# One block for attention, weight composition and feed-forward, with overlaid buffers and six early primitive pairs

## What is computed

```python
def _compose_weight(logits, A, B):
    vals, idx = jax.lax.top_k(logits, 32)
    w = jax.nn.softmax(vals)
    return jnp.einsum('k,kir,kro->io', w, A[idx], B[idx])
W1 = _compose_weight(fc1_logits, fc1_A, fc1_B)   # (256, 1024), rank 64
W2 = _compose_weight(fc2_logits, fc2_A, fc2_B)   # (1024, 256), rank 64
h = jax.nn.gelu(jnp.einsum('bsd,df->bsf', x, W1))
x = _layernorm(x + jnp.einsum('bsf,fd->bsd', h, W2))
```

## Time and profile before

| | us |
|---|---|
| median of 3 runs (lowest, highest) | 1985.33 (1983.23, 1987.44) |
| the profiled execution's own time | 1980.46 |
| its span, first to last instruction | 1978.6 |
| last attention output product to first composed pair, TensorE | 1091.8 to 1113.1 |
| composition, 32 pairs, TensorE | 1113.1 to 1214.0 |
| first product of the feed-forward | 1221.5 |

### The profile page before, as it was taken

The page is one execution under the profiler, slowest core; times in us unless marked ns, Lnnn a source line. Parts: engine busy times, 40 slices in busy tenths (PEclk is TensorE's granted clock), DMA queues, the critical chain, the costliest instruction groups (busy, mean ns, idle before and its releaser), DMA issues. The chain is left out here.

```text
span 1978.6 us, 47563 instructions
## 1 busy us (share of the span) xinstructions
PE 1921.4 (97%) x19760; PEld 1578.4 (80%) x19760; DVE 1344.3 (68%) x3293; ACT 981.7 (50%) x1803; POOL 1074.4 (54%) x1002
## 2 busy tenths in 40 slices
PE   8998999999999999999999699999999999999998
PEld 2335888888888888888888478999999999999997
DVE  3555566676667766776667465768696968677776
ACT  4454666676667666766676354223233232223231
POOL 1453998899888998899889111212222121313221
PEclk9997999999999999999999899999999999999999
DMA  7344200022000300021000694101010101010100
GB/s 273 122 162 166 105 34 34 34 76 76 34 34 8 112 34 34 34 76 55 34 24 20 187 239 102 43 22 43 22 44 33 38 28 44 22 44 22 44 11 22
DMA packets 26247, 128.04 MB, mean 65 GB/s; under 512 B 4592, under 2 KB 5168, under 8 KB 19888
## 3 DMA queue, kind: packets, MB, share of 16 engines
q1 hardware_dynamic: 17776, 78.08, 11.7%
q0 software_dynamic: 4624, 34.67, 5.7%
q10 hardware_dynamic: 3632, 12.26, 1.6%
HBM read 93.53 MB, written 31.46 MB: 63 GB/s over the span
## 5 line engine op out<-in xcount | busy, mean ns | idle before, releaser
L31 PE MATMUL bankC<-down_hi,act_hi 128*128 128x256 f32 x1024 | 289.5, 283 | 0.0
L33 PE MATMUL bankC<-down_hi,act_lo 128*128 128x256 f32 x1024 | 287.1, 280 | 0.0
L32 PE MATMUL bankC<-down_lo,act_hi 128*128 128x256 f32 x1024 | 286.9, 280 | 0.0
L1463 DVE TENSOR_TENSOR act_lo<-gel,act_hi 128x512 fp32r<-128x512 f32 x256 | 210.6, 823 | 8.8
L31 PE MATMUL bankC<-aT_hi,up_hi 128*128 128x512 f32 x512 | 204.9, 400 | 1.4 <-DVE aT_lo L1452 1.4
L1425 POOL TENSOR_TENSOR rstdC<-var_epsC,minus_halfC 128x4 f32<-128x4 f32 x48 | 53.6, 1117 | 278.4 <-DVE var_epsC L1488 278.4
L33 PE MATMUL bankC<-aT_hi,up_lo 128*128 128x512 f32 x512 | 202.1, 395 | 0.0
L32 PE MATMUL bankC<-aT_lo,up_hi 128*128 128x512 f32 x512 | 201.4, 393 | 0.0
L32 PEld LDWEIGHTS bankC<-down_lo,act_hi 128*128 128x128 f32 x1024 | 192.9, 188 | 1.4
L31 PEld LDWEIGHTS bankC<-down_hi,act_hi 128*128 128x128 f32 x1024 | 192.9, 188 | 1.4
L33 PEld LDWEIGHTS bankC<-down_hi,act_lo 128*128 128x128 f32 x1024 | 192.7, 188 | 0.0
(11 more groups left out here) (195 smaller groups left out, 5436.5 us busy)
## 6 DMA issues: line engine op xcount, KB each, us to landing
w_first<-w_split POOLq DMA_DIRECT2D x8, 1536.0 KB, 7.2
w_second<-w_split POOLq DMA_DIRECT2D x8, 1536.0 KB, 8.0
xs<-in_x_conv SPq DMA_DIRECT2D x16, 513.0 KB, 7.6
u<-hA SPq DMA_DIRECT2D x8, 1024.0 KB, 4.3
u_next<-u SPq DMA_DIRECT2D x8, 1024.0 KB, 5.4
u<-yB SPq DMA_DIRECT2D x8, 1024.0 KB, 4.6
hC<-u SPq DMA_DIRECT2D x16, 512.0 KB, 3.9
xC<-in_x SPq DMA_DIRECT2D x16, 512.0 KB, 4.2
```

Source lines behind the costliest of these rows:

```text
L31: e.matmul(out, wh, xh, start=start, stop=False)
L32: e.matmul(out, wh, xl, start=False, stop=False)
L33: return e.matmul(out, wl, xh, start=False, stop=stop)
L1463: e.tensor_tensor(a_lo[:, fb, :], g, a_hi[:, fb, :].bitcast(F32), ALU.subtract).then_inc(s_act_lo, 1)
```

## The change

- Attention, composition and feed-forward become one block. Each phase function returns its five engine programs (`Programs`), and each engine runs attention's, which then calls the next phase's. The wait of all engines between these phases is gone; instead an engine waits for named counts (`wait_free(w, before.free[...])`) before it uses memory that attention used.
- Buffers are laid over each other (`overlay`): three more raw buffers lie on the attention's tables `cos_k`, `sin_k`; `duo_hi` on `hT`; `duo_lo` on `gkT` and `kc`; `xC` and `hC` on `cos_q`, `sin_q`. PSUM: the first weight's banks are `ring`'s, the second's `big`'s; the feed-forward takes its banks in an order by which its first six are freed one after another.
- The ring of raw pairs has 6 buffers, all six loaded before the composition, three of them once the last unit's keys are rotated (`s_ks`). All halves are loaded by SyncE; GpSimd loads none.
- Unit 31 is finished between the pairs.
- ScalarE stores the last sequence after pair 11, and loads `b1s` and `vec` after pair 12, once that store has landed.
- Eight opening matmuls become four, ahead of pair 16; the first weight's banks are opened by their first matmul.
- The bias product comes after pair 22, and the first transposes and their split after pair 29.
- In `conv_phase`, three of the four semaphores of `band2` are shared with those of `band1`, so the first use of a part waits for both tables of it.

```diff
+            w.wait_ge(s_mul, 2 * (UNITS - PAIR + 1) + 2)
+            w.wait_ge(s_v, 4 * (UNITS - LANES))
+            prefetch(e, (0, 1, 2))
+            w.wait_ge(s_ks, 4 * UNITS)
+            prefetch(e, (3, 4, 5))
+            store(UNITS - LANES)
+            then(e)
...
+            def last(g):
+                if g == 0:
+                    copy_out(UNITS - 1)
+                    return
+                for o in range(4 * g - 4, 4 * g):
+                    unit(UNITS - 1, o)
+                if g == 2:
+                    w.wait_ge(s_unit, 8 * UNITS)
+                    n = UNITS - 1
+                    e.dma_start(rows_of(u_out, batch_of(n)), y_of(n)[:, :, :]).then_inc(d_sent[lane(n)], 16)
...
-                        if n == 5 + 4 * k + 2 * part:
+                        if n == 8 + 4 * k + 2 * part:
+                            wait_free(w, before.free["tables of q"])
...
-                    if n == 20 + 2 * s:
-                        e.wait_ge(d_u4[0], 16)
-                        e.dma_start(flat(hs[s]), pick(h_rows, 0, s)).then_inc(d_h[s], 16)
+                    if n == 26 + 2 * s:
+                        w.wait_ge(d_u4[0], 16)
+                        w.wait_ge(s_w_lo, 1)
+                        w.wait_ge(s_b1_ps, 1)
+                        e.dma_start(rows(hs[s]), pick(h_rows, 0, s)).then_inc(d_h[s], 16)
...
+            def scalar_loads(e, w):
+                wait_free(w, before.free["all"])
                 e.dma_start(b1s[:, :], b1).then_inc(d_consts, 16)
                 e.dma_start(vec[:, :], rows2.partition_broadcast(P)).then_inc(d_consts, 16)
...
+        FINISH = {2: 0, 3: 1, 4: 2, 6: 3, 7: 4, 8: 5}
+        UNITS_AT = {7: 1, 11: 2}
+        FIRST_AT = {14: 0, 22: 1}
+        TAKE_AT = DUOS + 2
+        BIAS_AT = DUOS + 6
+        ROWS_AT = len(duos) - 3
...
+            for n in range(RAW, len(duos)):
+                w.wait_ge(s_lo, n - RAW + 1)
+                for half in range(2):
+                    load_half(e, comp, picks, *duos[n], half, raw[n % RAW], d_raw[n % RAW])
+                first.sync(e, w, n)
...
+            wait_free(w, before.free["ring"])
+            for n in range(len(duos)):
+                if n == DUOS:
+                    w.wait_ge(s_zero, 1)
+                    wait_free(w, before.free["big"])
+                    for i in range(4):
+                        e.matmul(acc[1][i][:, :], zero[:, 0:P], zero[:, :], start=True, stop=False)
+                multiply(n)
+                if n == 0:
+                    last()
+                if n == BIAS_AT:
+                    w.wait_ge(s_out_lo, 4)
+                    first.tensor_bias(e, acc[0][0])
+                if n == ROWS_AT:
+                    w.wait_ge(s_out_lo, 4)
+                    rows()
...
+            wait_free(w, before.free["hT"])
+            for n in range(len(duos)):
+                prepare(n)
+                if n == 0:
+                    last(0)
+                if n in UNITS_AT:
+                    last(UNITS_AT[n])
+                if n == 12:
+                    first.scalar_loads(e, w)
+                if n in FIRST_AT:
+                    first.scalar(e, FIRST_AT[n])
+                if n == TAKE_AT:
                     take(0)
+            rows()
             take(1)
...
+        with nc.Block() as block:
+            block.sync(sync)
+            block.gpsimd(gpsimd)
+            block.tensor(tensor)
+            block.scalar(scalar)
+            block.vector(vector)
```

More of the change, by code:

```diff
@@ L1 @@
 import math
+from collections import namedtuple
 import concourse.bass as bass
@@ L1153, in ffn_phase @@
-def ffn_phase(nc, x, u_in, out, w1, b1, w2, rows2, comp, identity, w_col, picks, early, d_early, d_u4, x1_at, y_at):
+                invert(n)
+            key_value(UNITS - 1)
+            copy_turned(UNITS - 1)
+            then(e, lambda k: finish(UNITS - 1, k))
+        free = {"hT": [(s_v, 4 * UNITS)], "gkT, kc": [(s_kt, 4 * UNITS), (s_kr, 4 * UNITS)],
+                "tables of q": [(s_qr, 3 * UNITS), (s_qd, UNITS)], "ring": [(s_kvr, UNITS)], "big": [(s_y, 4 * UNITS)],
+                "all": [(s_unit, 8 * UNITS)] + [(d, 16 * (B // LANES)) for d in d_sent]}
@@ L1154, in ffn_phase @@
+        return Programs(sync, gpsimd, tensor, scalar, vector, free)
+def ffn_phase(nc, x, u_in, out, w1, b1, w2, rows2, comp, identity, w_col, picks, place, sems, before, early,
+              d_early, d_u4, x1_at, y_at):
     B, T, H = x.shape
@@ L1262, in ffn_phase @@
         aT = [split(f"aT{s}", [P, CB, TOK]) for s in range(LANES)]
-        act = [split(f"act{s}", [P, FB, TOK]) for s in range(LANES)]
+        act = [(place["act0_hi"], place["act0_lo"]), (place["act1_hi"], sb("act1_lo", [P, FB, TOK], F32R))]
         stats = sb("statsC", [P, LANES, TILES, 6])
@@ L1645, in scalar, with prepare @@
+        def scalar(e, last, rows):
             w = Waits(e)
-            first.scalar_loads(e)
-            def prepare(f, j):
-                n = duo_no(f, j)
+            def prepare(n):
+                f, j = duos[n]
                 r, q = n % RAW, n % SPLIT
                 w.wait_ge(s_mm, n - SPLIT + 1)
-                if n < len(early):
+                if n < RAW:
                     w.wait_ge(d_early[n], 2 * 16)
-                later = n // RAW + (r >= len(early))
-                for half in range(2):
-                    w.wait_ge(d_half[half][r], 16 * later)
+                else:
+                    w.wait_ge(d_raw[r], 2 * 16 * (n // RAW))
@@ L1695, in take, with overlay @@
                                     ALU.subtract).then_inc(s_out_lo, 1)
-            for f, j in duos:
-                prepare(f, j)
-                if (f, j) == (0, 10):
-                    first.vector(e, 0)
-                if (f, j) == (1, 2):
+            wait_free(w, before.free["gkT, kc"])
+            for n in range(len(duos)):
+                prepare(n)
+                if n in FINISH:
+                    last(FINISH[n])
+                if n in FIRST_AT:
+                    first.vector(e, FIRST_AT[n])
+                if n == TAKE_AT:
                     take(0)
-                if (f, j) == (1, 6):
-                    first.vector(e, 1)
+                if n == BIAS_AT + 2:
+                    first.vector_bias(e, acc[0][0])
+            rows()
             take(1)
-            first.vector_bias(e, acc[0][0])
-        with nc.Block() as block:
-            block.sync(sync)
-            block.gpsimd(gpsimd)
-            block.tensor(tensor)
-            block.scalar(scalar)
-            block.vector(vector)
+        free = [(first.done, 1), (s_out_lo, 4)] + [(s_out_lo, 4 + i) for i in range(1, 5)]
+        return Programs(sync, gpsimd, tensor, scalar, vector, free)
+def overlay(nc, stack, place, uses):
+    for use in uses:
+        own = stack if use is uses[-1] else ExitStack()
+        for name, shape, kind in use:
+            place[name] = own.enter_context(nc.sbuf_tensor(name, shape, kind))
+        if own is not stack:
+            own.close()
 def build(nc, t):
@@ new lines, in build @@
+        overlay(nc, ctx, place, [[("xC", [P, 2, T // P // 2, H], F32), ("hC", [P, 2, T // P // 2, H], F32)],
+                                 [("cos_q", split_rows, F32), ("sin_q", split_rows, F32)]])
+        d_u4 = [ctx.enter_context(nc.semaphore(f"d_u4_{s}")) for s in range(2)]
+        late = place["raw_late"]
+        early = [flat(u_next)[:, 0:width], w_flat[:, 0:width], w_flat[:, width:2 * width]] + [late[:, j, :] for j in range(3)]
+        d_early = [ctx.enter_context(nc.semaphore(f"d_early{j}")) for j in range(6)]
```

361 lines of the change are left out of this document (166 added, 195 removed).

## The result

| | before | after |
|---|---|---|
| median of 8 runs each (lowest, highest) | 1984.09 (1980.60, 1987.44) | 1974.70 (1971.98, 1977.99) |
| ratio, 95% interval | | 0.9955 (0.9944 to 0.9966) |
| the profiled execution's own time, span | 1980.46, 1978.6 | 1973.82, 1972.0 |
| end of unit 31's outputs | 1091.8 | 1090.8 |
| pair 0 starts on TensorE | 1113.1 | 1090.8 |

The change is 9.4 us faster. The forecast was 21.5 us, so the sign and the main mechanism held and the size did not: 1974.70 lies just outside the range of 1952 to 1974. The path from the end of the outputs to the feed-forward's first product went from 129.7 to 120.8 us, where 109.8 was forecast; and the feed-forward, forecast to keep its length, got longer.

A forecast was written before the change was run, and what follows sets the result against it. It took TensorE and DMA as two close limits in the composition. Terms summed to a path of 109.8 us against 129.7; with 1.6 from the feed-forward, 21.5 less than 1985.3: 1964 us, range 1952 to 1974.

The forecast's parts named there:

- The added wait on ScalarE: Composition, pairs 13 and 15: waits for the store, then `vec`, leave gaps of 4.4 and 3.2, together 7.6 us.
- I take 7: ScalarE's store of the last sequence: assumed to land 7 us after issue, so at 1130.0.
- rival 2: ScalarE's store queues behind SyncE's pairs and lands in 12.9: 13.5 instead of 7.6, total 1970 us; chance 0.20.
- Clock: TensorE in the composition: about 4 us at half clock after a gap cost 2.0 us, from nothing to 4.
- I count one: Clock losses in the composition: only one counted, 2.0 us; the first lies inside the wait of pair 15.
- It keeps its length: Feed-forward, TensorE busy from 1226 us: nothing the change touches runs there, so its 722 us stay unchanged.
- VectorE between pairs: Composition: in six places VectorE needs 3.1 to 3.4 against 2.77 us; costed at nothing, 1 to 2 without cover.
- SyncE's queue: SyncE waits for the bias product with pairs 27 to 31 queued behind: a gap of 1.6 us at pair 29.
- (1): Everything is covered: the store lands in 4, pairs are ahead, terms 7.6, 2.0 and 1.6 go; 1953 us, chance 0.12.
- (3): One queue carries less: SyncE alone moves 208 GB/s, 21.9 MB take 105.3 us; total 1973 us, chance 0.09.
- (4): Slower: SyncE's one queue moves only 164 GB/s, 133.5 us of transfer; total 2001 us, chance 0.03.
- (5): The gap only moves: pair 1 or freed buffers wait for unit 31; within 4 us of before, chance 0.03.

The follow-up runs named there:

- e6: Changed kernel with `b1s` and `vec` in memory of their own, loaded by SyncE with the early pairs, the store waited for after pair 14; 1959.72 us, ratio 0.9897.
- e4: Kernel before the change with only a 32-byte pad ahead of `act`, so `act` and `down` begin at the same place modulo 64; 1987.64 us, ratio 1.0024.
- e5: Changed kernel with `b1s` and `vec` in memory of their own, loaded by ScalarE without waiting for the store, which is waited for after pair 14; 1970.89 us.
- e7: As e6, with w1 rounded after pair 17 instead of 14; 1958.90 us, ratio 0.9886 to the kernel before the change.
- e9: Changed kernel with w2's halves loaded after pairs 20 and 22 instead of 12 and 14, and split at pair 26 instead of 22; 1968.96 us, ratio 0.9931.

## Why the prediction was right in kind and wrong in size

Its steps, against the changed kernel's trace:

| term | forecast us | measured us |
|---|---|---|
| wait ahead of pair 0 | 0.2 | 0 |
| 32 pairs | 90.6 | 90.9 (what is left of the path) |
| turn back and pair 1 | 2.4 | 2.3 (1093.65 to 1095.91) |
| idle ahead of pairs 12, 13, 15 | 0 + 4.4 + 3.2 | 1.3 + 7.9 + 7.3 |
| slow clock: pair 13, pair 15, behind the bias product | 2.0 | 2.0 + 1.5 + 1.5 |
| opening matmuls, bias product | 0.9 + 3.6 | 0.9 + 3.5 |
| gap ahead of pair 29 | 1.6 | 0 |
| transposes | 0.9 | 0.8 |
| gap ahead of pair 31 | 0 | 1.0 |
| path | 109.8 | 120.8 |
| the feed-forward's own length | 0 | +5.1 |

- **The added wait on ScalarE** is the step that failed by most: 7.6 forecast, 15.1 at pairs 13 and 15. The mechanism was right, both places and both releasers. The size failed in "I take 7" for the store and 6.6 for `vec`. The 6.6 came from a transfer issued with one of SyncE's ahead of it, and the earlier trace rows was read as showing that a later transfer is served at once. It showed the share once served. What the runs showed in its place is a wait for the first packet, 5.4 us for the store, followed by 4.9 us of transfer. The 7 did not follow from the forecast's own rule either: half of 244 GB/s is 122, so 1.05 MB take 8.6 us before any latency. Once served, the store had 68% of the engines, more than that half; rival 2's queueing was real too, but stopped after 5.4 us. The truth lay between the forecast and rival 2 for the store (10.3, between 7 and 12.9), and near rival 2 for `vec` (12.2). e6 confirms that these landings made the gaps: with `vec` loaded early and the store waited for only after pair 14, 12.5 us of idle time and slow clock went.
- **Clock**: the cost of one loss was about right, 1.5 to 2.0 us, but "I count one" failed: there were three, 5.0 us. Both gaps had one behind them. With the gaps forecast at 4.4 and 3.2, against the 1.96 us of the earlier trace rows behind which the clock had fallen, two should have been counted (gaps of about 2 us go either way: in e4 one of 2.10 had a loss behind it, 1.96 and 2.37 had none). The third came behind the bias product. The sum took the low clock of the transposes and of the cold start as gone, but what lies behind that product met it again in its new place, in all but one of the ten kernels with the new order. That the product causes it is read from rows; no run took it away.
- **"It keeps its length"**, said of the feed-forward, failed: +5.1 us. The argument was that nothing the change touches runs there. But the change touches where its operands lie, and a TensorE at 100% feels 1.7 ns a matmul. e4 shows it with a pad alone, 4.1 us in that stretch.
- **VectorE between pairs, costed at nothing**: 1.3 us at pair 12 and 1.0 at pair 31. Both came where GpSimd worked beside VectorE: GpSimd's two small operations after the last measurement took 1.51 and 1.56 us (0.24 and 0.23 on average before), and the norm's passes were waiting for them (the 1.75 us at 1121.71); and the subtraction of 2.61 us. The cover was thin by then, as ScalarE had waited 1.75 us for the load of pair 11, and 3.40, 1.31 and 1.78 us for those of pairs 29 to 31. Neither was taken away in a run, so these causes are read from rows only.
- **SyncE's queue** was priced too high: no gap at pair 29. The DMA's idle stretch was there, and the load of pair 29 was late for ScalarE by 3.40 us, but pairs were further ahead than assumed.
- **The start, the pairs, the opening matmuls, the bias product, the transposes** held within 0.2 us each, the pairs within 0.3.
- **Rivals.** (1) falls with the gaps ahead of pairs 13 and 15. (2) was the nearest in its mechanism, 1970 with the store at 12.9. (3) had the nearest number, 1973, and by luck: (3) and (4) fall, as SyncE's queue alone moved 1.38 MB in 6 us, 230 GB/s, as much as all queues did before. (5) falls with pair 0 at 1090.8.

The account closes on the profiled executions: path -8.9, attention ending 1.0 earlier, rest +3.4, together -6.6, and 1980.46 - 1973.82 = 6.6. The medians lie 9.4 apart, as the profiled execution of before was one of its fastest.

## What to carry to other kernels

When a change makes an engine wait for a transfer it has just issued, price the landing with what the other queue has outstanding at that moment, and count each link of a chain of landings; the cure is to issue the transfer when the DMA has less to do (e6), not to take away the wait alone (e5). When buffers are moved, a stretch that the change doesn't touch can still change its pace: compare start to start of the bound engine's matmuls before and after, and keep the operands where they were, relative to each other. And once a wait is gone, look at once for the next limit in the same stretch; here it was the DMA's bytes, and moving one megabyte to a slack stretch took the gap ahead of pair 15 away. Look at the granted clock by stretch too, also where the engine has no idle time: a loss of the clock that differs from trace to trace can hide what an edit gained, as in e7.

## What the runs showed of the hardware

- The store on ScalarE's queue, issued while SyncE's last outstanding transfer was 10.3 to 14.9 us from landing, had its first packet 5.0 to 5.7 us after its issue, in all ten kernels that have it. In e9 `vec`, with 4.9 us to that landing, had its first after 1.6. While the store ran, the two queues sent about as many packets each (97 and 106), so that the one with packets of 8 KB had 68% of the engines.
- With the stationary and the moving operand (128x256, fp32r) 32 bytes apart modulo 64, matmuls of lane 0 started 0.1167 to 0.1178 us apart, with both at the same place 0.1195 to 0.1199; in lane 1 the difference was 0.5 to 0.9 ns. Together it was 4 to 5 us in this kernel of 1975.
- A VectorE subtraction of 0.42 us took 2.61 beside a GpSimd addition, and GpSimd operations on 4 values a partition took 1.5 beside VectorE at work, against 0.23.
- At or behind a product of 32 matmuls of one column each, with no idle time before, the granted clock was 0.50 for 3.4 us in three kernels and for 6.8 in six, and did not fall in one; it cost 1.5 and 3.1 us.
